# Weighing a group's values in one unit instead of two, in a fused two-layer attention and expert kernel

## The reference, cut to what matters

```
layer 0 (16 heads, head size 8, values of size 16):
    att = softmax(causal(q1 k1 / sqrt 8)) - lam * softmax(causal(q2 k2 / sqrt 8))
    y = att @ v;  y = normalized per head;  s = y @ c_w
layer 1 (16 heads, head size 8, a window of 128 tokens):
    att = softmax(q k / sqrt 8 over the window);  s = (att @ v) @ wo.T + bo
both:
    x = x + s * silu(experts(xn))
```

## Time and profile before

| | |
|---|---|
| median of 3 runs | 1298.94 us |
| profiled execution, its own time | 1300.29 us |
| its span | 1298.1 us |
| TensorE matmuls | 1056.3 us (81%) |
| VectorE | 809.4 us (62%) |
| ScalarE | 799.4 us (62%) |
| reductions of scores, line 1438 | 576, 683 ns each |
| exponentials, line 1327 | 576, 598 ns each |
| weighing, 256 columns, line 1221 | 125.9 us busy |
| weighing, 128 columns, line 1224 | 78.8 us busy |

### The profile page before, as it was taken

One profiled execution on the slowest core, in us unless ns is written; L12 is line 12 of the kernel. 1 busy time (PEld: TensorE's weight loads), 2 busy tenths in 40 slices (PEclk: granted clock), 3 DMA queues, 4 the chain that ended last, 5 costly groups with the idle time before them and its releaser, 6 DMA issues. The chain is left out here.

```text
span 1298.1 us, 38266 instructions
## 1 busy us (share of the span) xinstructions
PE 1056.3 (81%) x12376; PEld 799.9 (62%) x12376; DVE 809.4 (62%) x1668; ACT 799.4 (62%) x1892; POOL 613.1 (47%) x918
## 2 busy tenths in 40 slices
PE   3349999489888789999899453599995999899995
PEld 3339999355555556655555343499993666566663
DVE  4676665477777667777774146656654777677741
ACT  4755555137877677777777543265552677677763
POOL 6256553012555455555565632665530345455554
PEclk9999999669999999999999855599995899899987
DMA  6502222422223313222220043022222222222210
GB/s 176 130 17 70 69 69 62 102 59 52 62 72 78 84 46 77 60 60 61 63 65 11 10 123 89 23 70 69 69 60 55 74 61 77 66 76 76 76 28 20
DMA packets 144613, 86.41 MB, mean 67 GB/s; under 512 B 16546, under 2 KB 138036, under 8 KB 144468
## 3 DMA queue, kind: packets, MB, share of 16 engines
q1 hardware_dynamic: 135828, 66.72, 19.8%
q0 software_dynamic: 8640, 17.71, 5.6%
HBM read 30.06 MB, written 15.60 MB: 35 GB/s over the span
## 5 line engine op out<-in xcount | busy, mean ns | idle before, releaser
L1438 DVE TENSOR_REDUCE at_maxima<-ps 128x2 f32<-128x512 f32 (+1 forms) x576 | 371.0, 683 | 188.5 <-PE ps L1131 185.1
L1327 ACT ACTIVATE at_probs<-ps 128x512 f32<-128x512 f32 x576 | 321.3, 598 | 68.9 <-PE ps L1131 64.6
L1130 PE MATMUL ps<-tables 64*128 64x256 bf16 (+1 forms) x2304 | 225.1, 256 | 86.1 <-DVE at_maxima L1438 39.6
L1131 PE MATMUL ps<-stack 62*128 62x256 bf16 (+3 forms) x3072 | 260.2, 251 | 2.9 <-issue 2.9
L717 ACT ACTIVATE ex_hid<-ps,ex_w 128x128 f32<-128x128 f32 x568 | 162.5, 369 | 120.2 <-PE ps L690 112.7
L1130 PEld LDWEIGHTS ps<-tables 64*128 64x128 bf16 x2304 | 89.5, 95 | 187.4 <-issue 156.3
L646 POOL DMA_INDIRECT ex_rows<-xn_rows,ex_ids_now x142 | 143.4, 1010 | 111.6 <-PE ps L681 68.8
L750 DVE COPY ex_w<-weights 128x1156 f32 x142 | 109.3, 770 | 104.1 <-issue 102.9
L1131 PEld LDWEIGHTS ps<-stack 62*128 62x128 bf16 (+1 forms) x3072 | 162.4, 98 | 13.6 <-issue 3.4
L1005 POOL DMA_INDIRECT at_chosen_y<-list_out,at_slot x128 | 129.6, 1012 | 55.3 <-issue 29.3
L690 PE MATMUL ps<-ex_rowsT,ex_w 128*128 128x128 f32 x1136 | 154.7, 280 | 0.0
(11 more groups left out here) (188 smaller groups left out, 1504.4 us busy)
## 6 DMA issues: line engine op xcount, KB each, us to landing
stack<-at_pieces SPq DMA_DIRECT2D x192, 128.0 KB, 2.8
stack<-at_pieces SPq DMA_DIRECT2D x192, 64.0 KB
list_out<-ex_result SPq DMA_DIRECT2D x142, 64.0 KB, 1.5
weights<-in_L_w SPq DMA_DIRECT2D x4, 1024.0 KB, 5.5
weights<-in_L_w SPq DMA_DIRECT2D x16, 256.0 KB, 6.5
xn_rows<-xn SPq DMA_DIRECT2D x8, 512.0 KB, 3.4
ex_rows<-xn_rows,ex_ids_now POOLq DMA_INDIRECT x142
x<-in_L_attn_x SPq DMA_DIRECT2D x4, 512.0 KB, 6.1
```

The lines of the kernel that those rows point to most:

```text
L1130: return nc.tensor.matmul(fine(bank, j), R.eye[tile, j, :], mask[tile], start=(j == 0), stop=True, skip_group_check=(j > 0))
L1131: return nc.tensor.matmul(bank[:, j - 2, :], left(j - 2)[tile], right(j - 2)[tile], start=False, stop=True, skip_group_check=True)
L1327: nc.scalar.activation(probs[:, (n // 3) % 2, n % 3, i * 512:(i + 1) * 512], t_bank[i], ACT.Exp, scale=SCALE).then_inc(t_free, 1)
L1438: nc.vector.tensor_reduce(by_half[:, h0:h0 + heads, a], s_bank[i].rearrange("p (m k) -> p m k", k=P * (late + 1)), AX.X, ALU.max).then_inc ...
```

## The change

Both parts of a group are weighed in the unit where part 1 was: units 4, 7, 10 and the next step's 1 in layer 0, units 4 and the next step's 1 in layer 1. The units before (3, 6, 9, 0) have their scores and general work alone. Nothing else is changed; no other engine's program differs.

```
-                    if n < 2 and has(step, "last"):
-                        weigh(step - 1, 1 - par, GROUPS - 1, n)
-                    if has(step, "now") and n >= 3 and n % 3 < 2:
-                        weigh(step, par, n // 3 - 1, n % 3)
+                    if n == 1 and has(step, "last"):
+                        for part in range(2):
+                            weigh(step - 1, 1 - par, GROUPS - 1, part)
+                    if has(step, "now") and n >= 3 and n % 3 == 1:
+                        for part in range(2):
+                            weigh(step, par, n // 3 - 1, part)
```

## The result

The changed kernel takes 1330.6 us in the median against 1298.1 for the kernel before on the same chip, a ratio of 1.0237 [1.0191, 1.0283]. One of its four executions took 1726.7 us at a granted clock of 0.569; the ratio goes by the other three (1324.6 to 1333.1), the median by all four. Its profiled execution took 1333.1 us, with a span of 1331.3 and a mean granted clock of 0.894 (before: 1300.3, 1298.1 and 0.911). So it is slower, by 33 us of span where the sum had 24.

A forecast was written before the change was run, and what follows sets the result against it. TensorE was taken to bound layer 0's units 1 to 8 and VectorE units 9 to 0. Terms 16.9 + 2.8 + 4.4 = 24.1 us on the profiled 1300.3 gave 1324.4, hence 1323 for the median; range 1306 to 1340.

The forecast's parts named there:

- the sum: Whole kernel: layer 0's and layer 1's costs add up to 24.1 us more; chance 0.43.
- a granted clock in layer 0 well below 1.00: Layer 0: named as a sign that the prediction is wrong, pointing to the clock falling.
- Its first rival: Layer 0, behind the 1.64 us idle before unit 10: clock falls in 8 of 13 steps, +14 us, 1337; chance 0.25.
- The price of a pair: Two parts side by side: 0.79 + 0.69 = 1.48 us, one changeover of 0.11 saved; bounds 1.37 to 1.58.
- Unit 9's part comes out of a hole: Layer 0, unit 9 loses 0.79 us of work: idle before unit 10 grows from 0.85 to 1.64, gain nothing.
- Unit 10's pair makes VectorE late: Layer 0, unit 10: unit 11's scores start 0.69 us later, so VectorE stands still and is 0.60 late.
- Unit 0's part comes out of VectorE's shadow: Layer 0: unit 0's loss gains nothing; the pair in unit 1 brings the total to +1.30 us a step.
- Units 2 to 8: Layer 0, forecast for units 3 to 8: +0.2 us a step for 14 steps, 2.8 us; bounds -4 to +6.
- Layer 1: Moves from unit 3 to 4 (zero) and 0 to 1: +0.37 us a step, 12 steps, 4.4 us; bounds 0 to 8.
- The rival of the gain: Whole kernel: TensorE is the bound where it matters, 96 changeovers of 0.11 saved, 10.6 us less, 1288; chance 0.10.
- The absorbed case: Layer 0, units 10 and 11: VectorE's lateness is absorbed, 13 x 0.69 = 9 us remain, 1308; chance 0.14.
- the cancelled case: Whole kernel: layer 0 costs 9 us, changeovers give 9, so 1299; chance 0.08.

The follow-up runs named there:

- group 3 alone: Against the kernel before, only layer 0's group 3 paired, its part moved from unit 0 to unit 1: 1312.1 us, 1.0100.
- group 2 alone: Against the kernel before, only layer 0's group 2 paired, its part moved from unit 9 to unit 10: 1322.0 us, 1.0183.
- groups 0 and 1 alone: Against the kernel before, only layer 0's groups 0 and 1 paired, parts moved from units 3 to 4 and 6 to 7: 1296.7 us, 0.9973.
- its repeat: The changed kernel timed again with no edit, beside the kernel before: 1328.0 us, 1.0233.
- the kernel with all pairs first: Against the changed kernel, both parts of every group in the first unit (3, 6, 9, 0 in layer 0) instead of the second: 1346.0 us, 1.0347.
- the kernel with only group 1 moved: Against the mixed kernel, group 1's pair of layer 0 in the first unit (6) too: 1285.2 us, 0.9887 to the kernel before.
- the mixed kernel: Against the changed kernel, pairs of layer 0's groups 2 and 3 and layer 1's group 1 in the first unit: 1284.9 us, 0.9874 to the kernel before.

## Why the prediction was right, point by point

The direction held, and so did the places where the order of the work costs time. The time, 1330.6, lies 7.6 above the 1323 forecast and inside the range, but that is in part luck: of the 31 us that the steps account for, the order makes about 11 and the clock, which the sum left out, about 20. The prediction itself had named a granted clock in layer 0 well below 1.00 as a sign of being wrong, and it is there: 0.94 from 490 to 660 us, 0.55 to 0.73 behind each hole. Its first rival, at 1337, is as near to the measured time as its sum. Step by step:

- **The price of a pair**, forecast 1.48: 1.44 at the full clock. One changeover saves 2 x 0.79 - 1.44 = 0.14, not 0.11.
- **Unit 9's part comes out of a hole.** The idle before unit 10 was to be 1.64 and is 1.63. Right, and its second effect, the clock, had been left to a rival.
- **Unit 10's pair makes VectorE late**, forecast 0.60: 0.45 where the clock stays up. **Unit 0's part comes out of VectorE's shadow**, and the pair in unit 1 is paid in full: group 3 alone adds 0.63. Together 1.30 was forecast a step (0.60, and 0.69 rounded with it), 1.04 was measured (0.41 by group 2 alone and 0.63). The places were right, the size a quarter too large, most of it in VectorE's lateness.
- **Units 2 to 8**, forecast +0.2 with bounds down to -0.3: -0.34, by groups 0 and 1 alone. This step failed in sign. Unit 6 begins 0.55 us sooner after unit 2 (7.68 us, 8.23 before): its idle of 0.28 is gone, a changeover (0.14) is saved, and unit 5's two banks follow each other 0.12 closer. The wait before unit 7 did appear, 0.37 in the changed kernel and 0.36 with only groups 0 and 1 paired, and from unit 6 to unit 9 0.21 is lost (7.53 us, 7.32 before). My sum let that wait eat up the gain before unit 6, because it took ScalarE's time from the earlier trace rows, and that step is not a usual one. There the exponentials of unit 6 begin 527.50 - 517.95 = 9.55 us after unit 2's scores; in the next step, and in most, 555.52 - 546.25 = 9.27 us after, and with the change 9.22:

```profile
517.95 0.39 PE L1130 MATMUL ps<-tables 64*128 64x256 bf16 x4
...
546.25 0.39 PE L1130 MATMUL ps<-tables 64*128 64x256 bf16 x4
```

```profile
555.52 1.09 ACT L1327 ACTIVATE at_probs<-ps 128x512 f32<-128x512 f32 x2
```

That is 0.28 of the 0.48 us between the +0.14 worked out for unit 7 and the -0.34 measured; 0.12 more is the lag to unit 7's second bank, taken as 0.26 and measured as 0.14 (from 671.91 to 672.05 in the changed kernel).

- **Layer 1**, forecast +0.37 a step: +0.18, and with the one step of a fallen clock gone, nothing that can be told from none remains (0.9991).
- **The clock**, left out of the sum and given a chance of 0.25 as the first rival. This is the term that made the sum too small: 1.55 us a step, in all 13 steps of the profiled execution (12 of 13 in its repeat) and not in 8. The evidence I set against it (the idles of 0.85 in layer 0 had no fall behind them) was right for idles of that length and said nothing on one twice as long; the trace of the kernel before did have one, of 1.66 us, with a fall behind it (277.31, above). The Trainium skill (TensorE: Matmul & The Clock Gate, Part 1) has the gate follow how busy TensorE has been, by a count that doesn't restart with the kernel; these traces fit it, with two equal holes of which one was followed by a fall, but no run here shows such a count.
- **The rival of the gain** is refuted as a whole: the changeovers are saved, and 0.14 each is even more than its price, but they come back only where TensorE is the bound. Groups 0 and 1 alone give 3.5 us, with an interval that all but reaches zero. The Trainium skill (TensorEngine Tiling (Array Packing), Key Properties) has TensorE drained at each change of tiling mode; the 0.14 agrees with that, and the slower kernel shows that a rule on one engine's throughput doesn't settle where its work should stand.
- **The absorbed case** happened to a quarter of VectorE's lateness (0.15 of 0.60), not to the whole; the cancelled case didn't happen.

The account of the span: in 13 steps 13 x (1.04 + 1.55 - 0.34) = 29.3. Read directly, the eleven steps between the output projections at 345.61 and 691.08 us (338.94 and 659.21 before) take 25.2 more, 2.29 a step. The first scores of layer 1 come 32.1 us later. These scores, before and after, by the timeline of TensorE:

```profile
988.59 0.61 PE L1130 MATMUL ps<-tables 64*128 64x256 bf16 x2 [7.90 <-DMA stack<-at_pieces]
```

```profile
1020.70 0.60 PE L1130 MATMUL ps<-tables 64*128 64x256 bf16 x2 [8.25 <-DMA stack<-at_pieces]
```

The 2.8 beyond the 29.3 fall outside those steps, in the filling and the last steps, taken at 0 to +3 in the forecast. Layer 1 adds 1.1.

So the forecast came near by two errors that partly cancelled, which is luck: it overstated the order's cost (24.1, where 13 x 1.04 - 14 x 0.34 + 12 x 0.18 = 13.5 - 4.8 + 2.2 = 10.9 by the measured sizes) and left out some 20 us of clock (13 x 1.55). The changed kernel with its hole filled, 10 us slower than before, is about what a right sum without the clock would have said.

**What stays open.** What the clock's fall depends on beyond the hole: in layer 0 one of 13 holes in the repeat and three of 13 with group 2 alone went without a fall, and in layer 1 of the kernel with all pairs first five of the last twelve of 1.64 us or more did. That a pair in unit 3 costs 17 us is shown; that it does so by making VectorE late for units 5 and 6 is read from the idles there and wasn't tested. With all pairs first there is also an idle of 1.02 us before unit 9, which the kernel with only group 1 moved shows too, without a loss in time. The last steps of layer 0, where the mixed kernel loses its clock, were not tried.

## What to carry to other kernels

Ask of each piece of work that is moved where it comes from: work that lies in an engine's idle time costs nothing there and its full length elsewhere, so a burst belongs in the hole and not behind it. In this kernel a hole in TensorE's work had a second price: behind most idles of 1.6 us the granted clock fell for the work that followed. That cost more than the order did, and putting useless matmuls in the hole was a quick test of it that gave back 17 to 19 us. Choose the place for each group of the pipeline apart, by which engine is late there: one rule for all gave +2.3% or +3.5%, a place for each -1.3%.

## What the runs showed of the hardware

- The clock fell in step with the loop, once in each step of 30.6 us, behind the idle of 1.63, to 0.59 in a stretch of 3.5 us (twelve times of thirteen in the repeat). The steps being alike, I had expected some to be hit and others not.
- More matmuls made the kernel faster, twice: 1328.0 to 1309.4 us in layer 0, 1322.0 to 1304.8 in layer 1.
- The price of a fall varied with the place: 1.5 us in layer 0, 1.6 to 3.2 us in a step of layer 1.
- The falls vary where the code doesn't: the kernel with group 3 alone has layer 1's code as it was, and yet after the filling four of its steps there take 17.8 to 19.4 us, where before one takes 17.85 and the usual one 16.3.
